# Routed expert rows added to the output by accumulating indirect stores, in place of a stage that combines them

## What is computed

```python
    h = _L0_tok_ref(x, L0_tok_W, L0_tok_b, L0_tok_cls_token, L0_tok_pos_embedding)
    h = jnp.concatenate([h, txt], axis=1)
...
        x_flat = x.reshape(B * T, C)
        router_logits = x_flat @ router_w.T
        router_probs = jax.nn.softmax(router_logits, axis=-1)
        top_k_probs, top_k_idx = jax.lax.top_k(router_probs, TOP_K)
        top_k_probs = top_k_probs / (top_k_probs.sum(axis=-1, keepdims=True) + 1e-08)
        cw = (jax.nn.one_hot(top_k_idx, E, dtype=x.dtype) * top_k_probs[..., None]).sum(axis=1)
        output = jnp.zeros_like(x_flat)
        for e in range(E):
            h = new_gelu(x_flat @ w1[e].T + b1[e])
            out_e = h @ w2[e].T + b2[e]
            output = output + cw[:, e:e + 1] * out_e
...
    h = h + _L1_ffn_ref(_layernorm(h, axis=-1), L1_ffn_router_w, L1_ffn_w1, L1_ffn_b1, L1_ffn_w2, L1_ffn_b2)
```

## Time and profile before

| | |
|---|---|
| Median of three runs | 1114.38 us (1110.06 to 1118.21) |
| The profiled execution | 1115.24 us |
| Its span, first to last instruction | 1113.4 us |
| TensorE's granted clock, mean | 0.907 |
| Busy time over the span | PE 932.3 (84%), DVE 569.7 (51%), ACT 574.5 (52%), POOL 620.6 (56%) |
| Routed stage, about | 782 to 1089 us |
| Combining stage | 1089 to 1113 us |

### The profile page before, as it was taken

How to read it: one execution, slowest core, us unless ns; L and a number is a source line. 1 busy time by engine, 2 the same in 40 slices (tenths; PEclk the granted TensorE clock), 3 DMA queues, 4 the chain that set the end, 5 groups by cost and what they waited for, 6 DMA issues and landing times. The chain is left out here.

```text
span 1113.4 us, 20955 instructions
## 1 busy us (share of the span) xinstructions
PE 932.3 (84%) x6700; PEld 843.5 (76%) x6700; DVE 569.7 (51%) x1280; ACT 574.5 (52%) x1201; POOL 620.6 (56%) x605
## 2 busy tenths in 40 slices
PE   6259699998699999969987999941699999999960
PEld 5248467776588988848886999941699999999960
DVE  1335489996555556338764465438233333333325
ACT  0021167776435656547645556630566666666640
POOL 0105658885625554435316998730477778778740
PEclk9669999998779999989997999965799999999985
DMA  7581234443011111100007000043466666666656
GB/s 250 163 296 51 65 134 149 164 147 138 1 58 58 58 58 58 58 1 1 2 1 310 1 15 24 20 180 151 143 189 195 206 194 201 193 191 200 200 154 244
DMA packets 64899, 137.04 MB, mean 123 GB/s; under 512 B 12505, under 2 KB 26578, under 8 KB 63490
## 3 DMA queue, kind: packets, MB, share of 16 engines
q1 hardware_dynamic: 55842, 113.34, 31.6%
q0 software_dynamic: 4848, 14.72, 3.8%
q10 hardware_dynamic: 4144, 8.16, 2.0%
HBM read 114.03 MB, written 24.39 MB: 124 GB/s over the span
## 5 line engine op out<-in xcount | busy, mean ns | idle before, releaser
L122 DVE CAST place<-place 128x512 fp32r<-128x512 f32 (+1 forms) x170 | 89.2, 567 | 166.8 <-PE moe_down L128 101.5
L2337 POOL TENSOR_TENSOR place<-place,place 128x512 fp32r<-128x512 f32 x84 | 138.1, 1644 | 51.5 <-DVE place L122 51.1
L2363 PE MATMUL moe_up<-place,place 128*128 128x128 f32 x1376 | 161.9, 276 | 0.0
L2363 PEld LDWEIGHTS moe_up<-place,place 128*128 128x128 f32 x1376 | 158.3, 193 | 0.0
L128 PE MATMUL moe_down<-place,place 128*128 128x256 f32 x1008 | 131.1, 286 | 0.4 <-POOL place L2337 0.4
L128 PEld LDWEIGHTS moe_down<-place,place 128*128 128x128 f32 x1008 | 123.4, 191 | 0.6 <-issue 0.6
L2422 ACT ACTIVATE place<-place 128x2048 f32 x44 | 84.0, 1912 | 43.6 <-PEq L2159 29.9
L2435 ACT ACTIVATE place<-moe_up,place 128x128 f32<-128x128 f32 x344 | 97.5, 366 | 13.5 <-POOL place L2337 13.2
L1425 POOL TENSOR_TENSOR place<-place,place 128x384 fp32r<-128x384 f32 x42 | 43.4, 1036 | 92.8 <-ACT place L1332 64.1
L787 PE MATMUL scores<-place,place 128*69 128x276 f32 x256 | 68.5, 412 | 11.1 <-DVE place L851 6.7
L1134 PE MATMUL ff_down<-place,place 128*128 128x256 f32 x486 | 70.7, 291 | 5.4 <-POOL place L1425 4.9
(11 more groups left out here) (273 smaller groups left out, 1987.2 us busy)
## 6 DMA issues: line engine op xcount, KB each, us to landing
place<-w_remainder SPq DMA_DIRECT2D x172, 256.0 KB, 3.8
place<-in_w_dram SPq DMA_DIRECT2D x4, 4096.0 KB, 13.3
place<-gate_rows SPq DMA_DIRECT2D x24, 384.0 KB, 4.8
place<-in_w_dram SPq DMA_DIRECT2D x16, 512.0 KB, 3.7
w_remainder<-place SPq DMA_DIRECT2D x16, 512.0 KB, 3.0
place<-value_rows SPq DMA_DIRECT2D x64, 64.0 KB, 2.3
place<-choices ACTq DMA_DIRECT2D x5, 768.0 KB, 8.4
place<-in_patches_dram SPq DMA_DIRECT2D x9, 384.0 KB, 4.1
```

What stands on the lines that cost most here:

```text
L122: return eng.tensor_copy(out, x)
L2337: pool.tensor_tensor(lo[f], raw[f], hi[f].bitcast(F32), ALU.subtract).then_inc(h_split, 1)
L2363: last = pe.matmul(p1[u][k // HK][:, (k % HK) * P:(k % HK + 1) * P], ws[u][:, c, k * P:(k + 1) * P], xT[u][:, c, :], start=(c == 0), stop= ...
```

## The change

There is no `combine` stage and no `choices` table. The output has 128 spare rows ahead of the 2304 padded token rows. `second_feed` writes `h` itself into the output, in six transfers of 384 KB beside those of `xn_rows`. The routed stage then adds each block's result rows to the output rows in place: the indirect store carries `compute_op=ALU.add`, so that a row is read, added to and written back. Rows that come together in the output have to be weighted before they are stored. For that, `xn_rows` has two more columns, the two weights of a token, which SP writes in the routing stage; the gather brings them with the row; and `weigh` picks by the slot's parity (first or second choice) the weight of each slot into `own`, by two VectorE operations of one column, three blocks ahead. `y` becomes (down result) x `own` + `w2_bw`, where `w2_bw` is the expert's bias times `own`, made by a further VectorE operation of 256 columns. `aim` computes the target rows: empty slots go to the 128 spare rows, one for each partition. The number of block columns in the tables goes from 44 to 46. SP's loop of remainder loads ends one block sooner.

```diff
-XBLK = NBLK + 2
+XBLK = NBLK + 4
...
-        self.xn_rows = self.dram("xn_rows", [NT * P, D])
+        self.xn_rows = self.dram("xn_rows", [NT * P, D + 2])
...
                     sp.wait_ge(unit[5], G * g + G)
-                    sp.dma_start(rows[:, G * g:G * g + G, :], of(x, g)).then_inc(xn_out, 16)
+                    sp.dma_start(rows[:, G * g:G * g + G, 0:D], of(x, g)).then_inc(xn_out, 16)
+                    sp.dma_start(out_rows[:, G * g:G * g + G, :], of(h, g)).then_inc(h_out, 16)
...
+                sp.wait_ge(weighed, 1)
+                sp.dma_start(self.xn_rows[:, D:D + 2].rearrange("(a p) k -> p a k", p=P), self.weight).then_inc(weights_out, 16)
+                sp.wait_ge(weights_out, 16)
                 sp.wait_ge(self.xn_out, 16 * NG)
+                sp.wait_ge(self.h_out, 16 * NG)
...
-                for w in self.weight:
-                    link(dve.tensor_tensor(w, w, total, ALU.mult))
+                dve.tensor_tensor(self.weight, self.weight, inner(total, 2), ALU.mult).then_inc(weighed, 1)
...
-                link(dve.tensor_copy(self.target, row))
-                link(dve.tensor_scalar(row, row, -1.0, 0.0, ALU.add, ALU.max))
-                link(dve.tensor_copy(self.source, row))
+                link(dve.tensor_scalar(past_row, row, -1.0, 0.0, ALU.add, ALU.max))
+                link(dve.tensor_copy(self.source, past_row))
+                link(dve.tensor_scalar(self.parity, self.source, 1, None, ALU.bitwise_and))
                 link(dve.tensor_scalar(self.source, self.source, 1, None, ALU.logical_shift_right))
...
-        self.choices = self.dram("choices", [1 + 2 * NT * P, D])
...
+                sp.dma_start(spare_row, t["spare_row"]).then_inc(spare_in, 16)
...
-                with sp.Fori(0, NBLK) as n:
+                with sp.Fori(0, NBLK - 1) as n:
...
                     pool.wait_ge(y_read, n + 1)
                     if n >= 1:
                         pool.wait_ge(stored[(n - 1) % 2], 16 * ((n - 1) // 2 + 1))
-                    pool.indirect_dma_start(out=self.choices, out_offset=bass.IndirectOffsetOnAxis(ap=self.target[:, n:n + 1], axis=0),
-                                            in_=y[n % 2], in_offset=None).then_inc(stored[n % 2], 16)
+                    pool.indirect_dma_start(out=self.out, out_offset=bass.IndirectOffsetOnAxis(ap=self.target[:, n:n + 1], axis=0),
+                                            in_=y[n % 2], in_offset=None, compute_op=ALU.add).then_inc(stored[n % 2], 16)
...
                         if f == 0 and n + 4 < XBLK:
                             pool.wait_ge(tx_mm, n + 3)
+                            pool.wait_ge(weighed, n + 3)
                             load(n + 4)
...
+                def weigh(n, i, u):
+                    dve.wait_ge(xg_in[u], i * 16 + 16)
+                    at = bass.ds(n, 1)
+                    dve.tensor_tensor(part[:, at], xg[u][:, D:D + 1], self.choice[0][:, at], ALU.mult).then_inc(parted, 1)
+                    dve.wait_ge(parted, n + 1)
+                    dve.scalar_tensor_tensor(out=own[:, at], in0=xg[u][:, D + 1:D + 2], scalar=self.choice[1][:, at], in1=part[:, at],
+                                             op0=ALU.mult, op1=ALU.add).then_inc(weighed, 1)
+                def aim():
+                    link = Steps(dve, aimed, 0)
+                    link(dve.tensor_copy(self.choice[1], self.parity))
+                    link(dve.tensor_scalar(self.choice[0], self.choice[1], -1.0, 1.0, ALU.mult, ALU.add))
+                    link(dve.tensor_scalar(where, self.slot_row, 1.0, None, ALU.add))
+                    link(dve.tensor_copy(self.target, where))
+                    link(dve.tensor_scalar(self.target, self.target, 1, None, ALU.logical_shift_right))
+                    link(dve.tensor_copy(where, self.target))
+                    link(dve.tensor_scalar(empty, self.slot_row, 0.0, spare_row, ALU.is_equal, ALU.mult))
+                    link(dve.scalar_tensor_tensor(out=where, in0=where, scalar=float(P - 1), in1=empty, op0=ALU.add, op1=ALU.add))
+                    link(dve.tensor_copy(self.target, where))
+                dve.wait_ge(spare_in, 16)
+                aim()
+                weigh(0, 0, 0)
+                weigh(1, 0, 1)
+                weigh(2, 1, 0)
                 split(0, 0, owner_of(dve, 0))
                 with dve.Fori(0, NBLK // 2) as i:
                     for u in range(2):
                         n = i * 2 + u
                         e, following = owner_of(dve, n), owner_of(dve, n + 1)
+                        weigh(n + 3, i + 1 + u, 1 - u)
                         dve.wait_ge(quarter_mm[3], n)
                         split(n, 1, e)
                         dve.wait_ge(quarter_mm[1], n + 1)
                         split(n + 1, 0, following)
+                        dve.tensor_scalar(w2_bw, w2_b[:, bass.ds(e, 1), :].rearrange("p a d -> p (a d)"), own[:, bass.ds(n, 1)], None,
+                                          ALU.mult).then_inc(biased, 1)
+                        dve.wait_ge(biased, n + 1)
                         dve.wait_ge(quarter_mm[3], n + 1)
                         dve.wait_ge(stored[u], i * 16)
-                        dve.tensor_tensor(y[u], p2[:, 0:D], w2_b[:, bass.ds(e, 1), :].rearrange("p a d -> p (a d)"), ALU.add).then_inc(y_read, 1)
+                        dve.scalar_tensor_tensor(out=y[u], in0=p2[:, 0:D], scalar=own[:, bass.ds(n, 1)], in1=w2_bw,
+                                                 op0=ALU.mult, op1=ALU.add).then_inc(y_read, 1)
...
-    def combine(self):
...
-                for k, (a0, a1) in enumerate(parts):
-                    n = tiles(a0, a1)[0]
-                    dve.wait_ge(got_in[k], 16)
-                    for a in range(a0, a1):
-                        for c in range(2):
-                            dve.scalar_tensor_tensor(out=self.h[0:n, a, :], in0=got[0:n, a, c, :], scalar=self.weight[c][0:n, a:a + 1],
-                                                     in1=self.h[0:n, a, :], op0=ALU.mult, op1=ALU.add).then_inc(mixed, 1)
-                            if c == 0:
-                                dve.wait_ge(mixed, 2 * a + 1)
...
-        self.combine()
...
-    out = nc.dram_tensor("out_0_dram", [N, D], F32, kind="ExternalOutput").ap()
+    out = nc.dram_tensor("out_0_dram", [P + NT * P, D], F32, kind="ExternalOutput").ap()
...
-    return result["out_0_dram"].reshape(NB, S, D)
+    return result["out_0_dram"][P:P + N].reshape(NB, S, D)
```

More of the change, by code:

```diff
@@ L1785, in second_feed @@
         halved = sem("sf_minus_half")
-        xn_out = self.xn_out = sem("xn_in_dram")
+        xn_out, h_out = sem("xn_in_dram"), sem("h_in_out")
+        self.xn_out, self.h_out = xn_out, h_out
         self.w1_in, self.w2_in = sem("moe_w1_in"), sem("moe_w2_in")
@@ L1810, in _ @@
                 rows = self.xn_rows.rearrange("(a p) d -> p a d", p=P)
+                out_rows = self.out[P:P + NT * P, :].rearrange("(a p) d -> p a d", p=P)
                 half = E * KF // 2
@@ L2139, in route_second @@
         self.source, self.target = m.take(XBLK).bitcast(U32), m.take(XBLK).bitcast(U32)
-        self.weight = [m.take(NT) for _ in range(2)]
+        self.parity = m.take(XBLK).bitcast(U32)
+        spent = self.lg.rearrange("p a e -> p (a e)")
+        self.slot_row, self.choice = spent[:, 0:XBLK], [spent[:, k * XBLK:(k + 1) * XBLK] for k in (1, 2)]
         self.owner = m.take(XBLK).bitcast(U32)
@@ L2154, in route_second @@
         rows = [m.take(NT * XBLK).bitcast(mybir.dt.bfloat16).rearrange("p (a g b) -> p a g b", g=2, b=XBLK) for _ in range(2)]
-        row = m.take(XBLK)
+        row, past_row = self.slot_row, m.take(XBLK)
+        self.weight = m.take(NT, 2)
         exped, step = sem("route2_exp"), sem("route2_step")
         hit, ranked, hot_ready, table_mm = sem("hits_ready"), sem("ranks_mm"), sem("slot_rows_ready"), sem("slot_table_mm")
+        weighed, weights_out = sem("route2_weights"), sem("route2_weights_out")
         lg = self.lg
@@ L2184, in _ @@
                 link(dve.tensor_tensor(lg, lg, inner(total, E), ALU.mult))
-                self.choose(lg, first, second, self.weight, tmp, dve, link)
+                self.choose(lg, first, second, [self.weight[:, :, k] for k in range(2)], tmp, dve, link)
                 link(dve.tensor_tensor(tmp, first, second, ALU.add))
                 dve.tensor_tensor(hits, tmp, inner(consts["valid"], E), ALU.mult).then_inc(hit, 1)
-                link(dve.tensor_tensor(total, self.weight[0], self.weight[1], ALU.add))
+                link(dve.tensor_tensor(total, self.weight[:, :, 0], self.weight[:, :, 1], ALU.add))
                 link(dve.tensor_scalar(total, total, 1e-8, None, ALU.add))
                 link(dve.reciprocal(total, total))
-                for w in self.weight:
-                    link(dve.tensor_tensor(w, w, total, ALU.mult))
+                dve.tensor_tensor(self.weight, self.weight, inner(total, 2), ALU.mult).then_inc(weighed, 1)
```

(6 more changed lines are left out.)

32 lines of the change are left out of this document (6 added, 26 removed).

## The result

The changed kernel takes **1135.22 us** (median of four runs, 1130.18 to 1136.23); the kernel before, run beside it, 1114.64 us. The ratio is 1.018, with a 95% interval of 1.015 to 1.021: 1.8% slower, where no change was forecast, and outside the range 1093 to 1119. The profiled execution took 1136.23 us, its span is 1134.2 us. The combining stage is gone. The routed loop got longer by twice what that saved.

A forecast was written before the change was run, and what follows sets the result against it. TensorE, busy throughout the routed loop (6.66 us a block), was taken as the bound, with the combining stage exposed. 1115.24 - 24.0 + 1.4 + 0.3 + 18.7 = 1111.6, forecast 1111 us (1105 to 1119; wider range 1093 to 1119).

The forecast's parts named there:

- Combining, -24.0: End of the kernel: the fully exposed combining stage of 24.1 us goes, its exit costing some 0.1 us elsewhere: -24.0 us.
- Accumulating store, +1.4: Routed stage's stores: reading old rows adds 0.7 us, hidden in the loop, counted twice at the end: +1.4 us (0 to 7.6).
- Routing and head, +0.3: Routing steps widen by 2 in 44 block columns, +0.3 us (0 to 0.6); `aim` and the first `weigh` cost nothing.
- weigh, 0.73 us: VectorE, between `y` and the next block's split: two chained operations and three register steps, 0.73 us (up to 1.10).
- The hold of the multiplication: VectorE ahead of `y`: GpSimd's subtraction holds the bias multiplication until 0.15 us before its end; `y` 0.96 or 0.86 us late.
- the failing step: Routed loop: after a stalled block the multiplication goes first, the next block does not stall, then the hold returns.
- the condition: Routed loop: a store or `weigh` together more than 0.5 us longer than taken lets the multiplication go ahead of GpSimd's subtraction.
- the 18.7 us: Routed loop: every second block stalls by 0.75 to 1.07 us, mean 0.91; 20.5 x 0.91 = +18.7 us.
- TensorE's room: Slack from the end of GpSimd's `lo[1]` to the second half of the down products: 0.84 and 0.62 us in alternate blocks.
- the first (no hold, 1094 us): Routed loop: the multiplication is not held and only `weigh` is left; 1094 us (1091 to 1104), chance 0.33.
- The second (stores set the period, 1144 us): GpSimd's queue: each store waits for the previous landing; with 2.5 us extra the period is 7.8 us, 1144 us; chance 0.12.

The follow-up runs named there:

- the last experiment: Changed kernel with multiplication and `weigh` both between the two splits, and a plain store in place of the accumulating one: 1087.70 us (0.977).
- the last two experiments: Changed kernel with multiplication and `weigh` both between the two splits, with accumulating stores (1089.26 us) and with plain stores (1087.70 us).
- the fastest version: Changed kernel with the bias multiplication and the loop's `weigh` both moved between the two splits: 1089.26 us (0.9775 of the kernel before).
- its two variants: The kernel before with a bias multiplication by 1.0 added on VectorE (1125.89 us), and the kernel before without its combining stage (1091.48 us).
- the two kernels with plain stores into the result: Plain store in the changed kernel (1117.15 us), and in the changed kernel with multiplication and `weigh` between the two splits (1087.70 us).

## Why the prediction was wrong

By its own steps:

- **Combining, -24.0.** Right (24.1 in the traces; 23.3 by the medians of the kernel without it).
- **Accumulating store, +1.4.** Wrong in sign. The tail from the last store but one is 3.5 us shorter: the two stores are 0.9 closer, the DRAIN is 3.0 shorter, and the rest is 0.4 longer. The landing itself is longer in the loop, where the page of the changed kernel gives 4.9 us for it; from the arrival events of the traces a plain store's is 3.9 before and 3.5 in the last experiment (means of 42). That is 1.0 to 1.4 us against the 0.7 taken, and 2.0 between the last two experiments; it is inside the bounds, and in the changed kernel no wait of the loop ends on it. What was given no price in the sum is the store's time on GpSimd: 1.59 us against 1.00.
- **Routing and head, +0.3.** No run shows the 0.3: the first gather lies between 779.1 and 785.6 us in the traces, whatever the edit. `aim` and the first `weigh` hold back the third gather (790.83 in place of 788.90), but in the fastest version they do so as well, and its first store comes 23.8 us behind the first gather, as before. The changed kernel's 2.0 us more between the first gather and the first store vary with the edit: 0.9 are left without the multiplication (24.7 us against 23.8), and two traces with the same loop differ by 0.6 (23.8, and 24.4 without the combining stage). How much of the 2.0 is the hold's is not shown.
- **weigh, 0.73 us.** Right as a size: from `y`'s start to the cast of the next split 2.57 us, 1.84 before.
- **The hold of the multiplication.** Found ahead of the run, with its cause and the right end (0.15 us behind GpSimd's). **Here the failing step stands**: "in a block that stalled [...] the subtraction is issued behind the copy's end, the multiplication goes first and `y` is in time", and with it the condition that more than 0.5 us of delay on GpSimd's side would end the hold. The delay came, 0.59 us by the store alone, and the hold stayed in every block: what counts is that the subtraction is ready, and the first copy makes it ready, always ahead of the second. A late store then does not free VectorE, it holds it longer. The size for one held block was near: with plain stores the kernel loses 0.70 us in every block, against the 0.91 that were expected in every second; the longer store adds 0.47. So the 18.7 us became 46.6, because the hold returns in every block and the two queues close into a circle, against which the prediction set only TensorE's room.

The sum with these sizes: 1111.6 + (46.6 + 2.0 - 18.7) - (1.4 + 3.5) - (0.3 + 0.2) = 1136.1, against 1136.2 measured. Of the rivals, the first (no hold, 1094 us) describes the kernel with the multiplication moved or left out (1092 to 1093 us); its condition, a store that takes 0.5 us more to issue, was met, and the hold did not go away by it. The second (stores set the period, 1144 us) came nearer to the time than the forecast, by another mechanism: GpSimd did not wait for its stores in the loop.

## What to carry to other kernels

An operation of 0.3 us in a queue that is 38% busy can cost more than three times its length in every turn of a loop, if another engine's operation holds it and a result that others wait for stands behind it; moving it one step up the queue gave back 1.08 of the 1.17 us a block. When two engines feed each other, add up the circle of their queues and compare it with the bound engine's period, since each link then counts almost in full (0.47 us for 0.50 of a store, 0.65 for 0.73 of two one-column operations). Where a forecast rests on who goes first, don't take the recorded starts: ask when each operation's last wait is satisfied.

## What the runs showed of the hardware

- An accumulating indirect store of 128 rows of 1 KB takes GpSimd 1.59 us in the changed kernel (up to 2.00 with the multiplication moved, where VectorE's wide copy starts late in it), a plain one 1.00 (up to 1.25 in the changed loop). It lands after 4.9 us, 5.5 in the fastest version (a plain one: 3.3 to 3.9).
- GpSimd's DRAIN at the exit of the stage takes 7.1 to 7.2 us behind plain indirect stores (7082 ns in the kernel before and its two variants, 7246 ns in the two kernels with plain stores into the result) and 4.1 us behind accumulating ones (4097 ns in all eight kernels that have them). The edit that only takes the addition out of the store changes it from 4097 to 7246 ns.
- VectorE's first copy of a split takes 0.7 and 1.0 us in turn in the changed kernel, in place of 0.43, when GpSimd's subtraction is under way.
- An operation of one column with both inputs in SBUF is held like a wide one (1.23 us in place of 0.16).
- A multiplication of 256 columns with its wide input in PSUM takes 0.47 us beside the subtraction; from SBUF it takes 0.34 us free and 2.40 us held.
